# Whole norms as two VectorE steps, a new order of side steps and opening, and two roundings moved, in a two-stage transformer kernel

## What is computed

```
mu  = x.mean(-1); var = ((x - mu)**2).mean(-1)
y   = (x - mu) * rsqrt(var + 1e-5) * g + b
first half:   x0  = norm(x) * (1 + scale1) + shift1               (norm "p")
  3 layers:   h   = norm(x + attention(x)) * ln1_g + ln1_b        (norm "1")
              x   = norm(h + relu(h W1 + b1) W2 + b2) * ln2_g + ln2_b  (norm "2")
              xp  = x_in + gate1 * x                               (after layer 3)
              x   = norm(xp) * (1 + scale2) + shift2               (norm "3")
second half:  2 layers, each with norm(shifted x) * ln_g + ln_b    (norm "f")
```

## Time and profile before

| | us |
|---|---|
| median of three runs | 3425.41 |
| profiled execution | 3431.81 |
| its span | 3429.9 |
| first half, to the first turn_tile | 1756.4 |
| TensorE busy | 2835.1 |
| VectorE busy | 2123.1 |
| GpSimd busy | 1921.7 |
| ScalarE busy | 1441.5 |

### The profile page before, as it was taken

The page is one execution under the profiler, slowest core; times in us unless marked ns, Lnnn a source line. Parts: engine busy times, 40 slices in busy tenths (PEclk is TensorE's granted clock), DMA queues, the critical chain, the costliest instruction groups (busy, mean ns, idle before and its releaser), DMA issues. The chain is left out here.

```text
span 3429.9 us, 61913 instructions
## 1 busy us (share of the span) xinstructions
PE 2835.1 (83%) x22184; PEld 2294.2 (67%) x22184; DVE 2123.1 (62%) x4931; ACT 1441.5 (42%) x3009; POOL 1921.7 (56%) x1732
## 2 busy tenths in 40 slices
PE   3698898989998988787627888898888889888886
PEld 1476776777776776676515677777667677767675
DVE  4556666665666665555435667666666766666664
ACT  1344344344353343333104554555545455545451
POOL 2356555555555556666655556555656655665653
PEclk7899999999999999999858899999999899999998
DMA  3000000010000010000020000000010100000000
GB/s 84 13 13 7 14 1 13 7 31 1 2 3 12 11 27 13 19 14 19 19 73 12 11 13 11 13 14 11 8 38 19 34 23 18 25 14 26 23 23 30
DMA packets 78001, 65.66 MB, mean 19 GB/s; under 512 B 15410, under 2 KB 72714, under 8 KB 77706
## 3 DMA queue, kind: packets, MB, share of 16 engines
q1 hardware_dynamic: 77706, 61.70, 6.1%
HBM read 49.10 MB, written 12.58 MB: 18 GB/s over the span
## 5 line engine op out<-in xcount | busy, mean ns | idle before, releaser
L967 ACT ACTIVATE PR<-PS,SM 128x256 f32<-128x256 f32 (+1 forms) x512 | 279.4, 554 | 444.3 <-DVE SM L1340 441.0
L858 ACT ACTIVATE FB<-PS,BC 128x512 f32<-128x512 f32 x192 | 132.1, 688 | 475.8 <-PE PS L250 475.2
L250 PE MATMUL PS<-WH,RH 128*128 128x256 f32 x768 | 230.9, 301 | 112.6 <-POOL RL L1566 110.2
L1728 POOL TENSOR_TENSOR OTL<-OO,OTH 128x512 fp32r<-128x512 f32 x64 | 82.4, 1288 | 359.0 <-ACT OTH L990 359.0
L250 PE MATMUL PS<-XTH,WH 128*128 128x512 f32 x576 | 251.7, 437 | 35.4 <-DVE XTL L1085 19.1
L1335 DVE CUSTOM_DVE_ANT_0 PS<-PS,MSK 128x256 f32<-128x256 f32 (+1 forms) x512 | 202.6, 436 | 116.1 <-PE PS L250 116.0
L1134 DVE TENSOR_TENSOR U<-PS,CST 128x512 f32<-128x512 f32 x384 | 238.2, 683 | 45.6 <-PE PS L250 45.5
L250 PEld LDWEIGHTS PS<-WH,RH 128*128 128x128 f32 x768 | 150.6, 196 | 154.7 <-issue 151.6
L1719 POOL TENSOR_TENSOR SM<-SM,COL 128x8 f32<-128x8 f32 x128 | 235.0, 1836 | 10.7
L250 PE MATMUL PS<-XTL,WH 128*128 128x512 f32 x576 | 232.9, 404 | 0.0
L250 PE MATMUL PS<-XTH,WL 128*128 128x512 f32 x576 | 231.9, 403 | 0.0
(11 more groups left out here) (212 smaller groups left out, 9165.0 us busy)
## 6 DMA issues: line engine op xcount, KB each, us to landing
PX<-in_L_attn_x SPq DMA_DIRECT2D x16, 512.0 KB, 3.9
TB<-in_k_rot SPq DMA_DIRECT2D x64, 128.0 KB, 2.1
SG<-in_L_attn_W SPq DMA_DIRECT2D x24, 256.0 KB, 2.8
xp_scratch<-PX SPq DMA_DIRECT2D x8, 512.0 KB, 2.9
xs_scratch<-X SPq DMA_DIRECT2D x64, 64.0 KB, 1.5
ZS<-xs_scratch SPq DMA_DIRECT2D x16, 256.0 KB, 2.9
GG<-xp_scratch SPq DMA_DIRECT2D x8, 512.0 KB, 4.1
out<-GG SPq DMA_DIRECT2D x8, 512.0 KB, 3.2
```

The lines of the kernel that those rows point to most:

```text
L250: return e.matmul(o, l, r, start=start, stop=True, skip_group_check=True)
L858: e.activation(FB[:, hb % 2, :], PS[:, 5, :], ACT.Relu, bias=BC[:, l % 2, 4 + hb:5 + hb]).then_inc(*a_re.up(n, hb))
L967: t = e.activation(PR[:, par, 256 * i + lo:256 * i + hi], PS[:, 3 + par, 256 * i + lo:256 * i + hi], ACT.Exp, bias=S[:, 40 + 2 * g + i:41 ...
L1728: e.tensor_tensor(OTL[:, :], OO[:, :], OTH[:, :].bitcast(F), ALU.subtract).then_inc(*h_ol.up(u))
```

## The change

1. Every norm is two VectorE passes. `centred`: (x - mean) * gain; it needs the mean alone, so it follows the statistics. `scaled`: * rstd + bias, after GpSimd's 1/sqrt. Both are `scalar_tensor_tensor`. GpSimd's gain1, bias1, second_norm, modulated, prologue passes and affine are gone. Norms "p", "1", "2", "3" take one statistics instruction per tile as before.
2. In layer 3, `gate_rows` multiplies ln2's gain and bias by the gate once per batch; `add_bias` adds the gated bias to the reloaded PX (one 128x1024 pass), and `scaled` adds PX as its bias.
3. First-half order: VectorE `rounded(m, 2)` before the value adds, `rounded(m, 4)` before the statistics of norm "1", RD and its reciprocal behind them; norm "3" and "p" end after `state(n, 3)`; GpSimd `low_hidden(m, 2)` and `(m, 4)` earlier, `add_bo` later; TensorE `key_sums` after `down(m, 3)`.
4. Opening: DMA order, modulation products in another order with two of six weight loads first, five of six copies on ScalarE, gate arithmetic inside step 0, weight splits spread by PLAN over steps 0 and 1 (and, for later layers, over their steps).
5. Second half: `centred` inside `norm_stats`, `scaled` as four 128x256 steps in `norm_apply`; `rounded2` of slots (3, 1) and (0, 1) moved behind `copy_p(u, 1)`.

```diff
+    PLAN = {(0, "v"): (3,), (0, "m0"): (4,), (0, "m1"): (5,), (0, "m2"): (6,), (1, "a"): (7, 8), (1, "v"): (9,), (1, "m0"): (10,), (1, "m1"): (11,)}
+    for b in (12, 24):
+        s = 8 * (b // 12)
+        PLAN |= {(s - 1, "m0"): (b,), (s - 1, "m1"): (b + 1,), (s - 1, "m2"): (b + 2,), (s, "m0"): (b + 3,), (s + 1, "m0"): (b + 4,),
+                 (s + 1, "m1"): (b + 5,), (s + 1, "m2"): (b + 6, b + 7), (s + 2, "a"): (b + 8, b + 9), (s + 2, "v"): (b + 10, b + 11)}
+    MODS = [(0, 0, 4), (1, 0, 5), (0, 1, 6), (1, 1, 7), (0, 2, 0), (1, 2, 1)]
...
-        def normed(key, outs, tiles):
+        def centred(key, outs, tiles, gain):
             a = ST[:, NORM[key] % 4, :]
+            e.wait_ge(*d_ag.at(*key))
+            for j, (o, t) in enumerate(zip(outs, tiles)):
+                t = e.scalar_tensor_tensor(out=o, in0=t, scalar=a[:, 48 + 2 * j:49 + 2 * j], in1=gain, op0=ALU.subtract, op1=ALU.mult)
+            t.then_inc(*d_na.up(*key))
+
+        def scaled(key, outs, tiles, biases):
+            a = ST[:, NORM[key] % 4, :]
+            e.wait_ge(*d_na.at(*key))
             e.wait_ge(*p_rs.at(*key))
-            for j, (os, parts) in enumerate(zip(outs, tiles)):
-                for o, part in zip(os, parts):
-                    t = e.tensor_scalar(o, part, a[:, 48 + 2 * j:49 + 2 * j], a[:, 56 + j:57 + j], ALU.subtract, ALU.mult)
-            return t
+            for j, (o, t, b) in enumerate(zip(outs, tiles, biases)):
+                t = e.scalar_tensor_tensor(out=o, in0=t, scalar=a[:, 56 + j:57 + j], in1=b, op0=ALU.mult, op1=ALU.add)
+            t.then_inc(*d_nb.up(*key))
...
                 statistics(("2", z), ztiles(z))
+                if z < 16:
+                    e.wait_ge(*s_row[4].at(z // 8))
+                else:
+                    e.wait_ge(*p_gr.at(1))
+                centred(("2", z), ztiles(z), ztiles(z), row(4) if z < 16 else MOD[:, (z % 8) // 4, D:2 * D])
+            if mlp:
+                rounded(m, 2)
...
+            if mlp:
+                rounded(m, 4)
+            if wo:
+                e.wait_ge(*d_z.at(w, 1))
+                statistics(("1", w), ztiles(w))
+                e.wait_ge(*s_row[2].at(w // 8))
+                centred(("1", w), ztiles(w), ztiles(w), row(2))
...
-                rounded2(q, hb)
+                if slot != 1:
+                    rounded2(q, hb)
+            if (i, slot) in ((3, 2), (0, 2)):
+                rounded2(q, what[(i, 1)])
...
+                for j, parts in enumerate(parts_of(q)):
+                    for i, part in enumerate(parts):
+                        o = ZS[:, j // 2, D * (j % 2) + 128 * i:D * (j % 2) + 128 * i + 128]
+                        t = e.scalar_tensor_tensor(out=o, in0=part, scalar=a[:, 48 + 2 * j:49 + 2 * j], in1=B2[:, 0, 128 * i:128 * i + 128], op0=ALU.subtract, op1=ALU.mult)
+                t.then_inc(*g_nc.up(q))
...
+                for j in range(4):
+                    o = tile_of(ZS, j)
+                    t = e.scalar_tensor_tensor(out=o, in0=o, scalar=a[:, 56 + j:57 + j], in1=B2[:, 1, :], op0=ALU.mult, op1=ALU.add)
...
             ffn(u, 1)
             if live:
                 copy_p(u, 1)
+            ffn(u, 2)
...
+        def add_bias(n):
+            b = (n % 8) // 4
+            e.wait_ge(*s_x.at("r", n))
+            e.wait_ge(*p_gr.at(b))
+            x = PX.rearrange("p i (t d) -> p (i t) d", t=2)
+            e.tensor_tensor(x, x, bcast(MOD[:, b, 0:D], 4), ALU.add).then_inc(*p_pb.up(n))
...
         for k in range(2):
-            for j in range(3):
-                e.dma_start(FQ[:, k, j, :], wm[:, k, 512 * j:512 * j + 512]).then_inc(*s_wm.up(3 * k + j))
+            e.dma_start(FQ[:, k, 0, :], wm[:, k, 0:512]).then_inc(*s_wm0.up(k))
+        e.dma_start(CST[:, :, :], ins["k_cst"]).then_inc(*s_cst.up(0))
+        e.dma_start(COL[:, :], ins["k_col"]).then_inc(*s_cst.up(1))
+        load_piece(0)
+        load_piece(1)
+        for k in range(2):
+            e.dma_start(FQ[:, k, 1:3, :], wm[:, k, 512:1536].rearrange("p (j n) -> p j n", j=2)).then_inc(*s_wm.up(k))
...
-        for p in range(3, 12):
+        for p in (3, 4):
+            load_piece(p)
+        load_x(2)
+        for p in (5, 6, 7, 8):
+            load_piece(p)
+        load_x(3)
```

More of the change, by code:

```diff
@@ L175, in build @@
     d_bs, d_ag, p_ve, p_rs = (ev(k, norms) for k in ("d_bs", "d_ag", "p_ve", "p_rs"))
+    d_na, d_nb = (ev(k, norms[:-NQ]) for k in ("d_na", "d_nb"))
     pieces = []
@@ L1171, in _ @@
-        e.wait_ge(*d_gate.at(5))
-        e.tensor_copy(CT[:, 0:1], CT[:, 12:13]).then_inc(*d_mod.up(8))
-        for p in range(3):
-            split(p)
+        prologue(0)
+        split(0)
+        split(1)
+        e.wait_ge(*e_mod.at(0))
+        e.tensor_copy(modulation(0, 0), PS[:, MODS[0][2], :]).then_inc(*d_mod.up(0))
+        e.wait_ge(*d_mod.at(0))
+        e.tensor_scalar(MOD[:, 0, D:2 * D], MOD[:, 0, D:2 * D], 1.0, None, ALU.add, ALU.bypass).then_inc(*d_mod.up(1))
+        e.wait_ge(*d_mod.at(1))
@@ L1261, in _ @@
                 masks(n, 1)
+            splits(n, "m1")
             if mlp:
@@ L1638, in _ @@
             l = n // 8
+            if z == 16:
+                gate_rows(0)
+                gate_rows(1)
             if mlp:
                 low_hidden(m, 0)
+            splits(n, "a")
+            if two:
+                rsqrt(("2", z))
+            if z in CH3:
+                add_bias(z)
             if live:
                 add_bo(n)
-            if n in (10, 18):
-                for p in (12 * l + 9, 12 * l + 11):
-                    split(p)
-            if two:
-                rsqrt(("2", z))
+            if mlp:
+                low_hidden(m, 2)
             if wo:
```

333 lines of the change are left out of this document (138 added, 195 removed).

## The result

The changed kernel takes 3057.3 us (median of 4 runs, 3052.8 to 3059.9) beside 3421.4 us for the kernel before on the same chip (median of 4): a ratio of 0.8933, 95% interval 0.891 to 0.8955. I had said 3125, with 3050 to 3220 around it: the sign and the range hold, and 68 us more were gained than my sum says. Span against span it is 3429.9 to 3056.7, 373.2 us less where I had added up 302.

The account below looks back on a forecast made before the run. The prediction took TensorE, busy 83%, to be held up by GpSimd in program order. Savings of 87 + 63 + 1 + 42 + 43 + 66 = 302 us from 3431.8 gave 3130, on the median 3124, stated as 3125; range 3050 to 3220.

Parts of the forecast that it names:

- the two for RL: Plain first-half step: TensorE's waits of 1.83 and 2.83 us for GpSimd's low words should both go, 4.7 us.
- Price of a norm step: Four new VectorE steps of 128x256 at 0.45 us each: 1.8 us a set, 3.6 us a norm, 2.2 more than before.
- Steps 2 to 18: First half: plain step 57.0 us, plus 2 on average for prologue norms and weight splits, 59.0; 87 us saved.
- The new wait: Plain first-half step: TensorE waits at sums(n,0) for VectorE's masks, 0 to 3 us, 1 us likely.
- Steps 19 to 23: First-half steps with longer norms: 57 + 3.5 = 60.5 us against 73.1; 63 us saved, bounds 50 and 75.
- Opening: Up to step 0's masks: they come at 54 us instead of 96.7; 42 us saved, bounds 34 and 46.
- Drain: Step 24 to the second half: 19 us from step 24, 5 from step 25, the rest after; 43 saved, bounds 33 and 50.
- Second half: Each of 16 quads: norms save 2.1 us net, moved roundings 2.0; 66 us saved, bounds 30 and 95.
- (a): VectorE bounds the first half: TensorE waits 3 us more at sums(n,0), clock drops; 3206 us; chance 0.20.
- (b): The clock recovers fully: steps go to 55 us, the second half saves 95; 3035 us; chance 0.10.
- (c): Slower than before: new VectorE steps take turns with GpSimd passes, 1.3 us each; 3583 us if half are blocked; chance 0.03.
- (d): The reordering ahead of step 0 starves on SP's queue, only the opening's gain goes: 3167 us; chance 0.09.

Follow-up runs that it names:

- e5_order: The kernel before with only the first half's new order, norms' gain and bias staying on GpSimd and the old opening kept: 3404.8 us, ratio 0.9952.
- e3_norms_old_order: The kernel after with the first half's order undone, its norms on VectorE, opening, weight splits and second half kept: 3098.2 us, ratio 0.9058.
- e4_splits_ahead: The kernel after with the splits of weight pieces 3 to 11 put ahead of step 0 again: 3066.8 us, ratio 0.8976.
- The two edits alone: The kernel before with only the second half's two roundings behind the copy of P (3363.0 us), or only its norms as two VectorE steps (3398.7 us).
- e6_extra_vector: The kernel after with four added VectorE passes on spare memory ahead of the masks in each of steps 1 to 24: 3098.8 us, ratio 0.9066.
- e1_roundings: The kernel before with only two of each second-half quad's roundings moved behind the copy of P: 3363.0 us, ratio 0.9834.
- e7_spare_passes: The kernel after with 14 GpSimd passes of 128x256 on spare memory added per step, nothing of the norms depending on them: 3141.9 us, ratio 0.9195.

## Why the prediction came out as it did

- **What bounds it.** Right: GpSimd in program order. The earlier trace rows named both of its chains; e5_order shows that the second one (VectorE's Z behind the second norm) stood right behind the first, and that removing the waits I had looked at most, the two for RL in the earlier trace rows, is worth 0.75 us a step by itself. I had put the gain of a plain step down to these two waits, 4.7 us; in the new kernel they are gone only because both chains are.
- **Price of a norm step.** 1.8 us predicted for a set of four, 1.67 measured; `centred` at 128 columns comes every 0.265 us, 2.1 for eight and not 2.6. The rows of the same operation at 512 columns and the straight line from the masks were good guides. The formula that the prediction took from the Trainium skill, VectorE: DVE Perf Modes (0.42 us at 256 columns, an estimate), met the step to the hundredth; that page's advice in "Rules for kernel authors" to keep the op count down was outweighed here: two ops a tile on VectorE for one, in a change that took 218 us off steps 2 to 23.
- **Steps 2 to 18: 134.8 us for 87, the largest miss.** The term that was mis-sized is the clock. A plain step is 55.5 and not 57.0. The new wait is 0.5 for my 1. For the clock I had taken off 0.8 us, half of what the earlier trace rows show as lost behind the second wait. In the windows of step 13, idle time falls by 4.8 us (my two waits were 4.7), and the same 512 matmuls take 1.7 us less, although 0.5 us of new wait is inside their time: so the clock gave back about 2.2 us, an estimate from these rows. (That step took 62.0 us, 0.5 more than the 61.5 from which I subtracted.) The other part of the miss, 1.3 us a step, is in the 2 us that I had added for prologues and splits: steps 2 to 18 average 56.2, only 0.7 above the plain one. They stand between the masks, where VectorE had 2 us of idle time a tile, and that cover held. Against eight steps like 11 to 14, the eight with splits were 31 us longer before and are 9 longer now. VectorE's chain of 18.5 us, where I had added up 17.8, has parts that I did not foresee: `scaled` 3.7 instead of 1.9, the scans 2.4 instead of 3.45, one low part RL 1.7 where it takes 0.7 alone. Under the old order (e3_norms_old_order) it is the scans that take 3.46 and `scaled` 1.66; one GpSimd pass is paid for by whichever of them stands beside it.
- **Steps 19 to 23: 83.1 for 63.** 56.4 a step, as short as the others, so the 3.5 us that I had added for the longer norms were covered the same way.
- **Opening: 47.7 for 42.** Both favor steps of the keys and queries run in one group from 35.5 us on (I had said 42 for the second), the masks at 48.3 (54). The gates' steps stand before them, as expected, and take 6.4 us. e4_splits_ahead gives 18 of the 48 us to the spread splits.
- **Drain: 33.4 for 43.** The one stretch forecast too high: the 31 us for step 24 left out TensorE's waits. Step 24, up to the Z add of step 25, takes 39.0 us: TensorE still waits 1.5, 2.4, 1.2, 1.9 and 2.2 us for low parts, 9.2 in all. Step 25 (26.5 for 27) and the tail (21.7 for 19.5) were near.
- **Second half: 70.3 for 66, a sum that came out by luck.** Its two terms were both off, in opposite directions. The two holes came out as I had said (1.8 and 0.8), but the roundings were worth 3.7 us a quad and not 2.0, since of 3.7 only 2.2 are idle time and 1.6 the same matmuls at a higher clock. The norms were worth 1.2 and not 2.1: the wait for the norm fell by 4.2 for my 4.9, the delay of the exponentials was 2.1 for my 2.8, and the hole of 1.2 us a quad more at the copy of P is the term that the sum lacked. (The two edits alone took 60 and 19 us, and the mean of the six traces with both is 77.5 below before; that the kernel after's own trace gained only 71.4 from OO to OO brought it nearer to my 66.)
- **Rivals.** (a), VectorE as the bound, was right in its mechanism and wrong in its size: e6_extra_vector shows it at the edge, with 0.5 us of wait where (a) had 3. (Its 3206 took the low end, 45, of the 44 to 77 us that its 2 to 3.5 us in 22 steps come to.) (b), the clock in full, happened in steps 2 to 18 and is one reason why the time lies toward it; in the second half the clock is 0.95, and the 95 us of (b) were 70. (Its sum was too small as well: 55 us in place of 59.0 and 60.5 is 95 us over 22 steps and not 60, so (b) as described comes to 3000 and not 3035.) (c) was there as single blocked sets (3.72, 4.80 us) but nowhere near the count that it needed. (d) did not occur: pieces and X came in time.

## What to carry to other kernels

Look behind the wait that ended last: removing it is worth only its lead over the next chain, and here that was another one through the same engine. When work moves off an engine that shares a port, price the relief of the neighbour's old instructions as well as the cost of its new ones, and where the clock had dropped behind a hole of TensorE, count the matmuls that get faster beside the hole (1.6 us for 2.2 of idle time in e1_roundings). Once two engines are level, every edit to a step belongs on the timeline of both: adding 2.0 us cost 2.0, removing 0.95 gave 0.5.

## What was not expected of the hardware

- A GpSimd power step on four or eight columns (1.1 and 1.7 us) does not slow VectorE's `scalar_tensor_tensor` beside it: in the kernel after, `centred` (from 2077.61) keeps its pace of 0.265 us through one of eight columns (from 2077.28, 1.66 us), and its set of 256 columns at 776.14 takes 1.67 us beside one of four. Only the wide passes, 0.7 to 1.3 us each, do.
- Two sets that shut each other out alternate, one VectorE step for each GpSimd pass: four VectorE steps of 0.4 us beside GpSimd passes of 0.73 us took 3.33 us (e7_spare_passes), beside four passes of 1.3 us 4.80 (kernel after, 2566.05).
- A pair of scans, whose inputs lie in SBUF, is as exposed as any: 3.45 us beside a GpSimd pass, 2.44 without.
